# Scores by key from float16 halves of the rotated queries and keys, in place of float32

## The reference, cut to what matters

```python
# x: 16 x 512 x 512, ctx: 16 x 120 x 512, 16 heads of 32
q, k, v = layernorm(x) @ Wq, ctx @ Wk, ctx @ Wv
qh, kh = rope(split(q)), rope(split(k))
score = einsum('bhqd,bhkd->bhqk', qh, kh) / sqrt(32)
x = x + (softmax(score) @ split(v)).reshape(...) @ Wo
# then a gated feed-forward over layernorm(x), with values rounded to 16 bits
# and weights to 4, each by the largest absolute value of its whole tensor
```

## Time and profile before

| | us |
|---|---|
| median of 3 runs | 2294.55 (2293.67 to 2299.99) |
| span of the profiled execution | 2290.3 |
| attention, from the start to about 744 | 744 |
| of it key and value projections, to step 9 | to about 168 |
| of it steps 14 to 22 | about 205 to 284 |
| of it a pattern of four steps, about 39 us long | 284 to 644 |
| feed-forward | about 744 to 2290 |

### The profile page before, as it was taken

One profiled execution on the slowest core, in us unless ns is written; L12 is line 12 of the kernel. 1 busy time (PEld: TensorE's weight loads), 2 busy tenths in 40 slices (PEclk: granted clock), 3 DMA queues, 4 the chain that ended last, 5 costly groups with the idle time before them and its releaser, 6 DMA issues. The chain is left out here.

```text
span 2290.3 us, 31254 instructions
## 1 busy us (share of the span) xinstructions
PE 2195.0 (96%) x12081; PEld 971.8 (42%) x12081; DVE 1689.5 (74%) x1696; ACT 1329.6 (58%) x1299; POOL 708.0 (31%) x655
## 2 busy tenths in 40 slices
PE   6998999999998999999999999999996899999999
PEld 3443333333333444444444444444443344444444
DVE  7757998898976666555532798888888787777773
ACT  3446666666654233223322978787876777778772
POOL 3645666666654211001100454343443000000000
PEclk9999999999999999999999999999998899999999
DMA  6444777777855677888775998777875466565552
GB/s 196 108 122 128 183 186 184 192 184 190 181 156 177 195 233 234 262 255 270 255 225 184 323 328 301 277 282 288 298 281 228 184 239 234 216 239 212 203 210 92
DMA packets 287191, 500.14 MB, mean 218 GB/s; under 512 B 187981, under 2 KB 190285, under 8 KB 250173
## 3 DMA queue, kind: packets, MB, share of 16 engines
q1 hardware_dynamic: 287036, 498.10, 67.9%
HBM read 247.75 MB, written 186.58 MB: 190 GB/s over the span
## 5 line engine op out<-in xcount | busy, mean ns | idle before, releaser
L1721 PE MATMUL banks<-XB,W 128*128 128x512 f16 x2304 | 498.1, 379 | 1.1 <-ACT XB L1747 0.8
L1721 PE MATMUL banks<-XB,WT 128*128 128x512 f16 x2304 | 497.4, 379 | 0.0
L2191 PE MATMUL banks<-W,OH 128*128 128x512 f16 x2256 | 488.7, 380 | 2.8 <-DVE OH L2297 2.8
L1741 ACT ACTIVATE OB<-banks,uns 128x512 f32<-128x512 f32 x384 | 255.4, 683 | 391.2 <-PE banks L1721 385.3
L1721 PEld LDWEIGHTS banks<-XB,W 128*128 128x128 f16 x2304 | 224.8, 98 | 274.1 <-DVE XB L1780 1.9
L1721 PEld LDWEIGHTS banks<-XB,WT 128*128 128x128 f16 x2304 | 225.1, 98 | 272.2
L2191 PEld LDWEIGHTS banks<-W,OH 128*128 128x128 f16 x2256 | 220.7, 98 | 270.6 <-DVE OH L2297 3.5
L2013 POOL TENSOR_TENSOR PR<-GS,OB 128x2048 f32<-128x2048 f32 x46 | 220.3, 4790 | 257.8 <-ACT OB L1741 247.8
L1830 DVE TENSOR_REDUCE amx<-OB 128x1 f32<-128x2048 f32 x48 | 109.7, 2285 | 237.6 <-ACT OB L1741 237.6
L770 PE MATMUL banks<-XC,AH 128*128 128x512 f16 x768 | 176.0, 380 | 8.4 <-POOL AH L1533 3.3
L711 PE MATMUL banks<-XD,WQ 128*128 128x512 f16 x768 | 177.0, 380 | 2.1 <-ACT QE L1021 0.8
(11 more groups left out here) (276 smaller groups left out, 2897.0 us busy)
## 6 DMA issues: line engine op xcount, KB each, us to landing
g_s<-OB SPq DMA_DIRECT2D x48, 1024.0 KB, 6.0
GL<-g_s SPq DMA_DIRECT2D x48, 1024.0 KB, 7.6
up_s<-OB SPq DMA_DIRECT2D x48, 1024.0 KB, 4.9
XA<-up_s SPq DMA_DIRECT2D x32, 1024.0 KB, 9.4
gq_s<-GQ SPq DMA_DIRECT2D x48, 512.0 KB, 4.9
XD<-gq_s SPq DMA_DIRECT2D x48, 512.0 KB, 6.7
XA<-in_x SPq DMA_DIRECT2D x16, 1024.0 KB, 6.3
QW<-QE SPq DMA_DIRECT2D x128, 128.0 KB, 3.1
```

The source lines that it names most:

```text
L1721: t = e.matmul(pk[:].rearrange("p (j t) -> p j t", j=4), WT[w][:, ot, wa, kk, :], XB[i % 2][:, xa, :, kk, :], start=(kk == 0 and wa == 0 a ...
L1741: e.activation(OB[n % 3][:, r, :], bank[(k + 4) % 8][:], ACT.Copy, scale=uns[:, 12 * w + ot:12 * w + ot + 1]).then_inc(s_ev, 1)
L2191: t = e.matmul(pk[:].rearrange("p (r n) -> p r n", r=4), OH[i % 2][:, a, ot, j * 128:(j + 1) * 128], WD[:, :, c, wa, o4, :], start=(ot == ...
```

## The change

- The rotated value is no longer kept in float32. The cosine product is made in place in QE, so it now waits for both DMAs that read QE. VectorE's sum also lands in QE.
- ScalarE then writes the high half, a float16 copy, into QR or KR (`act_rope_high`), and GpSimd writes the low half, sum less high half, also float16 (`pool_rope_low`). This is done for all 80 rotations, in the step after the one that made them (`halves_at`). `act_half` and its two copies per unit from unit 12 on are gone.
- Scores by key are three float16 products (high by high, high by low, low by high) in place of the float32 one. Scores by query take the high halves alone, in all units.
- QE has five buffers up to rotation 24 (the fifth is RB1) and four after it. A buffer is free when the low half of its rotation has been written (`s_rlo`). QR has six buffers in place of eight.
- The scales move: the query and key copies take a constant factor, and the exponential takes a factor from `cun`, one number for each partition.

```diff
@@ act_rope_in @@
-            if n >= 4:
-                before = n - 4 if n < 6 else n - 2
-                e.wait_ge(s_rm1, before + 1)
-                e.wait_ge(s_qw[n % 2], 32 * (before // 2 + 1))
...
+            if n >= 5:
+                e.wait_ge(s_rlo, qe_before(n) + 1)
+
+        def act_rope_high(e, n):
+
+            what, i = ROTS[n]
             e.wait_ge(s_radd, n + 1)
...
+            if what == "q" and i >= NQ:
+                e.wait_ge(s_c1, i - NQ + 1)
+            e.activation(rot_half(n, 0), qe(n)[:, 0:rot_width(n)], ACT.Copy).then_inc(s_rhi, 1)
@@ act_attention @@
-                if HALF <= s - 1 < NU:
-                    act_half(e, s - 1)
+                for n in halves_at(s) if s != 1 else []:
+                    act_rope_high(e, n)
                 for nb in x_at(s, 2) if s >= 16 else []:
                     act_x_high(e, nb)
                 if s == 1:
                     act_split(e, 2)
                     act_ctx(e, 1)
+                    for n in halves_at(s):
+                        act_rope_high(e, n)
                 for i in kv[:1]:
                     act_kv(e, i)
@@ pe_scores @@
-            for g in range(4):
-                e.matmul(PB[0:SK, g, :], KR[g0][32 * g:32 * g + 32, c, bb * SK:(bb + 1) * SK], QR[u % 8][32 * g:32 * g + 32, :],
-                         start=True, stop=False)
+            e.wait_ge(s_rlo, ROT["q", u] + 1)
+            e.wait_ge(s_rlo, ROT["k", 8 * g0 + c] + 1)
+            for n, (ka, qa) in enumerate(((0, 0), (0, 1), (1, 0))):
+                for g in range(4):
+                    e.matmul(PB[0:SK, g, :], KR[g0][32 * g:32 * g + 32, ka, c, bb * SK:(bb + 1) * SK],
+                             QR[u % NQ][32 * g:32 * g + 32, qa, :], start=(n == 0), stop=False)
@@ pool_rope_cosine @@
-            if what == "q" and i >= 8:
-                e.wait_ge(s_c1, i - 7)
-            e.tensor_tensor(to, v(qe(n)), cc, ALU.mult).then_inc(s_rm1, 1)
+            e.wait_ge(s_qw[n % 2], 32 * (n // 2 + 1))
+            e.tensor_tensor(v(qe(n)), v(qe(n)), cc, ALU.mult)
...
+        def pool_rope_low(e, n):
+
+            e.wait_ge(s_rhi, n + 1)
+            e.tensor_tensor(rot_half(n, 1), qe(n)[:, 0:rot_width(n)], rot_half(n, 0), ALU.subtract).then_inc(s_rlo, 1)
@@ pool_attention @@
                 for u in normal_at(s):
                     pool_normal(e, u)
+                for n in halves_at(s):
+                    pool_rope_low(e, n)
                 if s < NU:
                     pool_rope_cosine(e, ROT["q", s])
                     pool_rope_sine(e, ROT["q", s])
```

More of the change, by code:

```diff
@@ L73, in now_at, with halves_at @@
     return tiles_at(s)[:2] if s in (4, 6) else []
+def halves_at(s):
+    if s < 2:
+        return [0, 1] if s == 0 else [2, 3, 4]
+    return tiles_at(s - 1) if s <= NU else []
 def normal_at(s):
@@ L288, in build @@
         cq, sq = sbuf(st, "cq", [128, 512]), sbuf(st, "sq", [128, 512])
-        KH = [W0[:, 12000 + SK * i:12000 + SK * (i + 1)] for i in range(2)]
         ck, sk = (W0[:, 11520 + 2 * SK * i:11520 + 2 * SK * (i + 1)].bitcast(FP32) for i in range(2))
```

128 lines of the change are left out of this document (56 added, 72 removed).

## The result

| | kernel before | changed kernel |
|---|---|---|
| median | 2296.25 us (2293.67 to 2299.99) | 2327.87 us (2324.74 to 2331.30) |
| span of the profiled execution | 2290.3 | 2322.9 |

The ratio is 1.0147, with a 95% interval from 1.0133 to 1.0161: the changed kernel is 1.5% slower, some 32 us. The forecast was 17.5 us slower. The direction was right, and the size was about half of what came.

The account below looks back on a forecast made before the run. TensorE sets the pace from 192 to 284 us, with VectorE at 322.65 of 360 from 284 to 644. Stops +23.5, clock +3, savings -7 -3.5 -2, long stretch +3.5 make +17.5: 2312 us, range 2284 to 2335.

Parts of the forecast that it names:

- The first stop: Copy of q1 waits for low half 0, until 48.9; unit 0's scores by query start at 60.0, 5.1 us later.
- The second stop: q1's rotation on GpSimd behind three low halves; scores by query at 73.1, q4's projection at 85.8; loss now 12.5 us.
- Steps 4, 5 and 7: ScalarE's bank-emptying copies stand behind high halves that wait for additions; TensorE loses 3, 5 and 3 us.
- The clock: Behind some four more stands of 3 us or longer the granted clock falls: 3 us lost, from 0 to 7.
- Off again: Gains from cheaper products: 7 us scores by query, 3.5 scores by key of steps 7 to 22, 2 from 644 on.
- The later part: From 284 to 644 us, low halves and late cosine cost 0.4 us for each of nine patterns, +3.5.
- I call it even: Second step of a pattern, cosine 1.27 us later: the addition runs about 0.9 shorter or waits 1 us; no net cost.
- the long stretch: 284 to 644 us, patterns of four steps, VectorE busy 322.65 of 360; a faster TensorE gains nothing there.
- The third rival: GpSimd becomes the bound from 284 to 644 us: 2.5 us a pattern, nine times 22, 2334 us; chance 0.16.
- The sum again: Whole kernel: +23.5 + 3 - 7 - 3.5 + 3.5 - 2 = +17.5 us on the span of 2290.3.
- the things to look for: Signs in the trace: q1 copy near 49, q4's projection near 86, four-step patterns 39 to 39.5 us, GpSimd 107 us busier.

Follow-up runs that it names:

- e4_warm: The changed kernel with TensorE filling five of its early waits with identity products nobody reads: 2320.20 us, ratio 1.0101.
- e13_slowpe: The changed kernel with TensorE's savings taken away: high-by-high product made twice, scores by query of units 0 to 11 three times; 2325.98 us, ratio 1.0141.
- e18_rest: The changed kernel with 8 columns of every low half, six buffers, own cosine buffer from step 11, warming products ahead of three projections: 2305.06 us, ratio 1.0051.

## Why the prediction was wrong in size, point by point
**The first stop: right.** The copy of q1 at 48.9 came at 49.06, the scores by query of unit 0 at 60.0 came at 60.16.

**The second stop: right within 3 us.** The projection of q4 came at 83.76 in place of 85.8, a loss of 10.5 and not 12.5. Unit 1's scores by query came at 76.05, not 73.1; the projection ahead ran at half clock.

**Steps 4, 5 and 7: each there, two of them too small.** I had 3, 5 and 3 us, and nothing for 6, 8 and 9. The offset of the scores by query rose by 7.2 (unit 2 to 3), 4.6 (3 to 4) and 7.0 (5 to 6), and fell by 3.3 up to unit 9. Half clock behind the stops is in these figures. By the scores by key the offset stood at 28.9 in step 8, where 23.5 and 3 are 26.5: stops and clock were 2.4 us too small. That the balance at step 11, 25.4, is close to 26.5 is luck, since 3.5 us of TensorE's saving had come off by then.

**The clock: direction right, size open between 3 and 10.** Five stops, not four, and 2 to 2.7 us more for the products behind each; e4_warm returned 10 us by the ratio and 2 to 3 by the offsets. A sixth stop, in step 14, was not in the forecast at all, and the clock behind it was 0.50 for 6 us.

**"Off again", -12.5 us: wrong, the first step that failed.** The credit of 7 for nine cheap scores by query, 3.5 for the scores by key of steps 7 to 22 and 2 behind 644 supposed that TensorE sets the pace there, as it seems to before. The runs show 3.5 us of it, in steps 8 to 11, and no more: e13_slowpe took the saving away in all steps and the time stayed, 1.0141 against 1.0147. In the steps before, the stops in the same sum had taken the pace from TensorE, and from step 14 on it stands 9 us in eight steps where it stood 2.8. That this is why the rest of the credit never came is read from the traces; no run puts the saving into the kernel before by itself. I had priced stops and savings as if both could count at once.

**The later part: wrong in steps 14 to 22, the second.** I had let the low halves and the late cosine cost 0.4 us a pattern from 284 on, and had nothing for them in steps 14 to 22, only the credit. The 0.4 was about right: the growth from unit 15 to 57 is 4.5 us on average where I had 3.5, and a pattern of four steps from unit 15 to 55 is 38.2 us in the kernel before, 38.2 in the shown execution of the changed one and 38.5 in the second. "I call it even" did no harm. The step that failed is that steps 14 to 22 got no cost for the same work: there the growth is 5.2 us, 3.6 of them at the stop of step 14, where the cosine behind the landing makes GpSimd, then ScalarE and then the query copy late, and the clock falls. I had followed a pattern of the long stretch by its waits and none of these steps. e18_rest, with low halves and cosine both off the path, has 0.3 us there (9.9 to 10.2). The third rival (GpSimd becomes the bound, 2334) came nearer in time than the forecast, but its mechanism, 2.5 us in each pattern, is not there.

**The sum again.** 25.4 us at step 11 in place of 19.5 (23.5 + 3 - 7), which is 2.4 more of stops and clock and 3.5 less of credit, then 2.6 off at step 14, then 10.1 more to step 70 in place of -2 (-3.5 + 3.5 - 2): 32.9 in place of 17.5. Of the things to look for, GpSimd is 92.5 us busier (800.5 against 708.0), not 107, for a low half takes 1213 ns and not 1369.

## What to carry to other kernels
A saving on the engine that sets the pace and a new wait on the way to it don't add: find which of the two ends last in each stage, and credit the saving only there. A cost worked out for one stage has to be worked out for its neighbours too. To price work given to an engine with idle time, put the same work into the unchanged kernel where nobody waits for it; that one run says what its idle time is worth at that place in its queue, though not what it is worth in the changed kernel. When a stop is removed by reordering, look for what was late behind it before counting it as gain.

## What I had not expected of the hardware
Products of the identity in a wait went with a granted clock of 1.00 through 71 to 76 us (0.56 without); at 114 us, where 3.14 us of the wait were left over, it was 0.56 with them too. GpSimd's instructions beside VectorE's with float16 results were nearly twice as long: the cosine and sine of step 14 in the changed kernel took 2.40 and 2.24 us where they take 1.27, with VectorE making the low halves of a weight and of x from 227.39 to 234.15:
```profile
228.47 2.40 POOL L1497 TENSOR_TENSOR QE<-QE,cq 128x512 f32<-128x512 f32 x1 [1.01 <-DMA QW<-QE]
230.82 2.24 POOL L1506 TENSOR_TENSOR QW<-QW,sq 128x512 f32<-128x512 f32 x1
233.03 3.69 POOL L1541 TENSOR_TENSOR AH<-A,AH 128x512 f16<-128x512 f32 x2
```
```profile
235.25 0.60 ACT L1018 ACTIVATE A<-banks 128x512 f32<-128x512 f32 x1 [4.25 <-POOL AH L1541]
```
ScalarE then waited 4.25 us for GpSimd. The Trainium skill, SBUF — State Buffer, Who interferes with whom, has it that the two engines lock each other out of a shared pair of ports; the trace agrees in kind, but no run here took that contention away alone. And the exponential takes 1960 ns with a scale read from a tile for each partition, 1869 with a constant one, in the groups of the long stretch.
